# Decay sums read back from device memory instead of picking products, and the state's product in two column tiles

## The reference, cut to what matters

```
dt  = softplus(dt + dt_bias);  dA = dt * (-exp(A_log))        # per token and head, 8 heads
A_cs = cumsum(dA)                                             # over the tokens of a chunk
Lmat = exp(A_cs[l] - A_cs[s]) for l >= s, else 0
Y_diag = sum_s (C_l . B_s) Lmat[l, s] xdt[s]                  # xdt = x * dt
states = sum_s B_s exp(A_cs[-1] - A_cs[s]) xdt[s]
S = S * exp(A_cs[-1]) + states
Y_off  = (C_l . S_before) * exp(A_cs[l])
```

## Time and profile before

| | |
|---|---|
| median of 3 runs | 996.51 us (996.26 to 999.14) |
| profiled execution | 1000.16 us, of which span 998.4 us |
| PE / DVE / ACT / POOL busy | 91% / 79% / 60% / 34% |
| mean granted TensorE clock | 0.97 |

### The profile page before, as it was taken

One profiled execution on the slowest core, in us unless ns is written; L12 is line 12 of the kernel. 1 busy time (PEld: TensorE's weight loads), 2 busy tenths in 40 slices (PEclk: granted clock), 3 DMA queues, 4 the chain that ended last, 5 costly groups with the idle time before them and its releaser, 6 DMA issues.

```text
span 998.4 us, 17980 instructions
## 1 busy us (share of the span) xinstructions
PE 909.1 (91%) x6560; PEld 786.0 (79%) x6560; DVE 789.2 (79%) x2079; ACT 599.2 (60%) x1013; POOL 338.6 (34%) x346
## 2 busy tenths in 40 slices
PE   1556797999999999999999999999999999999987
PEld 0445695888888788888888798878888798888887
DVE  6898777898879988898879988898879888886132
ACT  5955847574737665674737565674838565672222
POOL 2022233334252424334152424234152524234332
PEclk9767799999999999999999999999999999999999
DMA  7300000000001000000001000000000000000000
GB/s 225 124 1 11 1 12 1 12 11 2 11 2 32 1 12 1 11 23 1 12 1 33 1 11 1 11 23 1 12 1 33 2 11 2 5 18 1 1 22 11
DMA packets 14087, 17.70 MB, mean 18 GB/s; under 512 B 1712, under 2 KB 10416, under 8 KB 14000
## 3 DMA queue, kind: packets, MB, share of 16 engines
q1 hardware_dynamic: 13136, 16.53, 5.4%
q10 hardware_dynamic: 864, 0.03, 0.0%
HBM read 12.36 MB, written 4.19 MB: 17 GB/s over the span
## 4 chain that ended last, share of the span: by engine, by line
PE 58%; DVE 22%; ACT 7%; issue 6%; POOL 5%; DMA 1%; SPq 1%; DVEq 0%; POOLq 0%; ACTq 0%
PE fb L1073 23%; PE mb L1073 14%; PE db L1073 11%; DVE xc L882 7%; PE mb L1193 2%; DVE lmat L856 2%; DVE hid L990 2%; DVE lmat L901 2%; POOL yg L557 2%; DMA wd_raw<-in_packed 1%; PE mb L1174 1%; PE mb L1199 1%; PE mb L1184 1%; POOL hl L569 1%; ACT xc L651 1%
## 5 line engine op out<-in xcount | busy, mean ns | idle before, releaser
L569 POOL TENSOR_TENSOR hl<-hid,hl 128x512 fp32r<-128x512 f32 (+1 forms) x144 | 169.5, 1178 | 407.9 <-ACT hl L705 407.7
L1073 PE MATMUL fb<-x1t,wg 128*128 128x512 f32 (+1 forms) x864 | 215.9, 386 | 5.3 <-DVE x1t L984 5.3
L1073 PE MATMUL db<-wd,hl 128*128 128x256 f32 x1536 | 216.6, 289 | 2.2 <-POOL hl L569 2.0
L1073 PEld LDWEIGHTS db<-wd,hl 128*128 128x128 f32 x1536 | 197.4, 189 | 17.8 <-issue 10.1
L1073 PE MATMUL fb<-x1t,wu 128*128 128x512 f32 (+1 forms) x864 | 206.1, 375 | 3.3 <-ACT hid L698 3.3
L1073 PEld LDWEIGHTS fb<-x1t,wu 128*128 128x128 f32 x864 | 153.6, 192 | 36.7 <-ACT hid L698 4.8
L1073 PEld LDWEIGHTS fb<-x1t,wg 128*128 128x128 f32 x864 | 146.3, 193 | 30.9 <-DVE x1t L984 6.7
L990 DVE TENSOR_TENSOR hid<-fb,hid 128x512 f32<-128x512 f32 (+1 forms) x144 | 90.2, 627 | 78.1 <-PE fb L1073 67.6
L705 ACT ACTIVATE hl<-hid 128x512 fp32r<-128x512 f32 (+1 forms) x144 | 83.6, 581 | 106.1 <-DVE hid L990 77.8
L882 DVE SCALAR_TENSOR_TENSOR xc<-raw,cw,xc 128x256 f32<-128x256 f32 x288 | 132.9, 529 | 9.6 <-ACT xc L651 8.3
L698 ACT ACTIVATE hid<-fb 128x512 f32<-128x512 f32 (+1 forms) x144 | 78.1, 548 | 84.8 <-PE fb L1073 81.1
(11 more groups left out here) (150 smaller groups left out, 1360.4 us busy)
## 6 DMA issues: line engine op xcount, KB each, us to landing
xin<-in_u SPq DMA_DIRECT2D x16, 256.0 KB, 2.7
out<-xb SPq DMA_DIRECT2D x16, 256.0 KB, 2.2
wg_raw<-in_packed SPq DMA_DIRECT2D x4, 256.0 KB, 13.2
wg_raw<-in_scales SPq DMA_DIRECT2D x4, 256.0 KB
wu_raw<-in_packed SPq DMA_DIRECT2D x4, 256.0 KB, 13.6
wu_raw<-in_scales SPq DMA_DIRECT2D x4, 256.0 KB
wd_raw<-in_packed SPq DMA_DIRECT2D x4, 256.0 KB, 13.2
wd_raw<-in_scales SPq DMA_DIRECT2D x4, 256.0 KB
```

The source lines that it names most:

```text
L569: pool.tensor_tensor(hl[:, hs, n % 2, 1, :], hid[:, hs, n % 2, :], hl[:, hs, n % 2, 0, :].bitcast(F32), ALU.subtract).then_inc(s["lo"], 1)
L1073: last = pe.matmul(ps, lhs(a, k), rhs(b, k), start=start and n == 0, stop=stop and n == len(todo) - 1, skip_group_check=check)
```

## The change

1. `pick`, `t3`, `seg` and their products go. `da` is now 128 wide with 16 filled columns, `decays` is one copy of the sums from PSUM to `csr` in SBUF, and `ct` is one float32 product of `csr` with 16 columns of the identity, into the same bank as `cs`.
2. SP stores the 16 rows of `csr` (8 KB) in device memory, waits until they have landed, and reads them back twice, 8 rows each (4 KB), each read spread over all 128 partitions straight into `lmat` (512 KB each). It does so for each half in its own queue, between the loads of x and the stores of the result.
3. `sums` waits for both reads and takes the last column from `lmat`, one instruction more. `decay_sums` works in place in `lmat`, so it reads SBUF and not PSUM.
4. `st` is two matmuls of 64 output partitions each.
5. The Mamba table has 42 uses of the three banks in place of 52.

```diff
@@ ORDER["pe"] (FIRST likewise)
-        gu:0< cs:0 gu:1< ct:0 gu:2< dn:0< gu:3< dn:1< seg:0 seg:1 seg:2 dn:2< xtr:0 gu:4< gb:0 yo:0 seg:3 gu:5<
+        gu:0< cs:0 gu:1< ct:0 gu:2< dn:0< gu:3< dn:1< dn:2< xtr:0 gu:4< gb:0 yo:0 gu:5<
...
+            def spread_rows(i, j):
+                if not there("cs", j, i):
+                    return
+                n = halves_before(i, j)
+                sp.wait_ge(s["cs_read"], count("cs_read", i, j))
+                sp.dma_start(rows[n % 2], csr[0:2 * HEADS, :]).then_inc(rows_stored, 16)
+                sp.wait_ge(rows_stored, 16 * n + 16)
+                for c in range(2):
+                    if n == 0:
+                        sp.wait_ge(wi_ready, 2)
+                        sp.wait_ge(wi_z_ready, 1)
+                    else:
+                        sp.wait_ge(s["yd"], count("yd", i, 2 * j + c - 2))
+                    sp.dma_start(lmat[:, c, :, :].rearrange("p h l -> p (h l)"),
+                                 rows[n % 2, HEADS * c:HEADS * c + HEADS, :].rearrange("h l -> (h l)").partition_broadcast(P)
+                                 ).then_inc(rows_spread[c], 16)
...
+            for i in range(NBLK + 1):
+                for j in range(2):
+                    spread_rows(i, j)
+                    next_x(i, j)
+                if i > 0:
+                    store(i - 1, (i - 1) % 2)
...
             def decay_sums(i, par, k):       # ACT; DVE likewise
-                act.wait_ge(s["ct_read"], count("ct_read", i, k // 4))
-                if h0 == 0:
-                    wait_before(act, "yd", i, k // 2 - 2)
-                act.wait_ge(s["seg"], count("seg", i, k))
+                act.wait_ge(s["sums"], count("sums", i, k // 4))
...
-                    last = act.activation(lmat[:, c, h0 + h, :], m_bank["seg", k][:, CH * h:CH * h + CH], ACT.Relu,
+                    last = act.activation(lmat[:, c, h0 + h, :], lmat[:, c, h0 + h, :], ACT.Relu,
...
             def decays(i, par, j):
-                ps = m_bank["cs", j][0:96, 0:CH]
                 dve.wait_ge(s["cs"], count("cs", i, j))
-                link("cs_link", i, 3 * j, dve.tensor_copy(t3[:], ps))
-                dve.tensor_tensor(rest3[0:64, :], ps[0:64, :], t3[0:64, :], ALU.subtract).then_inc(s["cs_read"], 1)
...
+                if halves_before(i, j) > 0:
+                    dve.wait_ge(rows_stored, 16 * halves_before(i, j))
+                dve.tensor_copy(csr[:], m_bank["cs", j][:, 0:CH]).then_inc(s["cs_read"], 1)
             def sums(i, par, j):
...
+                dve.tensor_copy(ct_[:, 0, :], m_bank["cs", j][:, CH:CH + 2 * HEADS]).then_inc(s["ct_read"], 1)
+                for c in range(2):
+                    dve.wait_ge(rows_spread[c], 16 * halves_before(i, j) + 16)
+                dve.tensor_copy(ct_[:, 2, :].rearrange("p (c h) -> p c h", c=2), lmat[:, :, :, CH - 1])
                 dve.wait_ge(s["ct_read"], count("ct_read", i, j))
...
             def ct(i, par, j):
...
+                pe.matmul(m_bank["cs", j][:, CH:CH + 2 * HEADS], csr[:], ident[:, 0:2 * HEADS], start=True,
                           stop=True).then_inc(s["ct"], 1)
...
-                pe.matmul(m_bank["st", q][:], gb[:, 2 + c, :], xdd[:], start=True, stop=True).then_inc(s["st"], 1)
+                for n0 in range(0, NSTATE, HD):
+                    last = pe.matmul(m_bank["st", q][n0:n0 + HD, :], gb[:, 2 + c, n0:n0 + HD], xdd[:], start=True, stop=True)
+                last.then_inc(s["st"], 1)
```

More of the change, by code:

```diff
@@ L181 @@
                 decays=1, ct=1, sums=1, exps=1,
-                seg=4, decay_sums=4, decay_matrix=4, ip=3, taps=3, conv=3, silu=3, z=3, gate=3, gb=1, gb_copy=1,
+                decay_sums=4, decay_matrix=4, ip=3, taps=3, conv=3, silu=3, z=3, gate=3, gb=1, gb_copy=1,
                 decayed_products=2, xtr=2, xdt=2, yo=2, yoff=2, yd=2, st=2, state=2, ydiag=2, square=2, yt=2,
@@ L278, in build @@
         yt = sb("yt", [P, 2, KI, CH], F32R)
-        da = sb("da", [P, 3, 32])
-        t3 = sb("t3", [96, CH], BF16)
-        rest3 = sb("rest3", [96, CH])
+        da = sb("da", [P, CH])
+        csr = sb("csr", [P, CH])
         ct_ = sb("ct_", [P, 3, 2 * HEADS])
@@ L331, in build @@
         out_stored = sem("out_stored")
+        rows_stored = sem("rows_stored")
+        rows_spread = [sem(f"rows_spread{c}") for c in range(2)]
         small_loaded = sem("small_loaded")
@@ L362, in build @@
             var4=1, rstd4=1, d_read=1, outs=2,
[L363 removed]
+            ln1_link=4, dt_link=12, conv_link=30, out_link=24, fin_link=3)
         s = {name: sem("s_" + name) for name in per_block}
@@ L398, in drive, with halves_before @@
             run(LAST[engine], NBLK, 1)
+        rows = nc.dram_tensor("rows", (2, 2 * HEADS, CH), F32, kind="Internal").ap()
+        def halves_before(i, j):
+            return 2 * i + j - 1
         u_v = u.rearrange("b (h c p) d -> (b h) p c d", c=2, p=P)
@@ L460, in load_x, with next_x @@
                 sp.dma_start(xin[:, j, :, :], src).then_inc(x_loaded[j], 16)
[L462 to L467, removed]
+            def next_x(i, j):
+                if there("ln2", 2 * j + 1, i + 1) and (i, j) != (0, 0):
+                    sp.wait_ge(s["attn"], count("attn", i, 2 * j + 1))
+                    load_x(i + 1, j)
+            def spread_rows(i, j):
[14 more added lines that the diff above has]
+                                 ).then_inc(rows_spread[c], 16)
             load_x(0, 1)
-            rows = in_proj.rearrange("(k p) n -> p k n", p=P)
-            sp.dma_start(wi_raw[:, :, DI:], rows[:, :, DI:]).then_inc(wi_loaded[0], 16)
-            sp.dma_start(wi_raw[:, :, 0:DI], rows[:, :, 0:DI]).then_inc(wi_loaded[1], 16)
+            wi_rows = in_proj.rearrange("(k p) n -> p k n", p=P)
+            sp.dma_start(wi_raw[:, :, DI:], wi_rows[:, :, DI:]).then_inc(wi_loaded[0], 16)
+            sp.dma_start(wi_raw[:, :, 0:DI], wi_rows[:, :, 0:DI]).then_inc(wi_loaded[1], 16)
             for q in range(MATS * PIECES):
@@ L515, in consts @@
                 pool.memset(hist[:], 0.0)
-                pool.memset(upto[:], 1.0)
                 pool.memset(da[:], 0.0)
-                link(pool.memset(pick[:], 0.0))
+                link(pool.memset(upto[:], 1.0))
                 pool.affine_select(out=upto[:], in_=upto[:], compare_op=ALU.is_ge, fill=0.0, base=0,
[L521 to L528, removed]
+                                   pattern=[[1, P]], channel_multiplier=-1).then_inc(consts_ready, 1)
             def wi_split(i, par, _):
@@ L1113, in cs @@
                 bank_read(m_uses, ("cs", j), i)
[L1114 to L1115 removed]
+                pe.matmul(ps[:, 0:CH], da[:], upto[:], start=True, stop=True).then_inc(s["cs"], 1)
             def ct(i, par, j):
[L1118 to L1121 removed]
+                pe.wait_ge(s["cs_read"], count("cs_read", i, j))
+                pe.matmul(m_bank["cs", j][:, CH:CH + 2 * HEADS], csr[:], ident[:, 0:2 * HEADS], start=True,
                           stop=True).then_inc(s["ct"], 1)
[L1124 to L1132 removed]
             def z(i, par, q):
```

66 lines of the change are left out of this document (17 added, 49 removed).

## The result

The changed kernel takes 1000.07 us (median of 20 runs, 998.49 to 1002.18). Beside it the kernel before took 996.33 us (20 runs, 994.57 to 1000.89). The ratio is 1.0034, 95% interval 1.0026 to 1.0043: slower by 2.6 to 4.3 us. Its profiled execution took 1001.04 us, with a span of 999.3 at a mean granted clock of 0.967 of full speed.

The account below looks back on a forecast made before the run. PE was taken to bound most of an iteration, DVE one first-half stretch and the second half to `yt:2`. Start +8.1, iterations -3.9, step 8 -1.3, semaphores +0.6 gave +3.5 on 996.5: 1000.0 us, range 988 to 1020.

Parts of the forecast that it names:

- The landing, 7.3 us: Copy to `csr`, store and both reads: the sums lie in `lmat` 7.3 us after `decays` starts; ends 6.4 and 11.4.
- Rival A: Read-back into `lmat`: spread reads slow, 190 GB/s, data 5.5 us not 3.1; +36, about 1036 us; chance 0.14.
- Start +8.1: Start's three halves: rows 3.2 us late each, `sums` 0.2 longer, partly paid back later; 8.1 us, ends 5 and 20.
- First half of an iteration: no stall: DVE's wait for the rows: reads land by 544.4, DVE asks at 544.7 or later; 0.3 to 1.1 us to spare.
- Second half +0.4: Iteration's second half to `yt:2`: +0.5 stall, +0.2 `sums`, +1.1 POOL, -1.0 `decay_sums`, -0.4 waits; PE's relief unused.
- POOL's collision, +1.1: Second half: one `decay_sums`, now reading SBUF, is held about 1.1 us by POOL's `hl`.
- First half -1.3: Iteration's first half: -0.8 `decays`, -1.0 `decay_sums`, +0.2 `sums` make -1.6, counted as -1.3; ends 0 and -2.9.
- The state's tiles +0.25: State's product on PE: tiles run side by side, 0 behind `yd`, +0.25 us at `st:3` for mode changes.
- Rival C: State's product on PE: column tiles do not run side by side, +0.86 x 3 an iteration; 1015 us; chance 0.12.
- Iteration -0.65, tail -1.3, total +3.5: Whole program: six iterations -3.9, step 8's first half -1.3, start +8.1, semaphores +0.6; together +3.5 us.
- PE idle before `yt:2`: Sign of the prediction in an iteration's second half: PE would idle before `yt:2`, waiting for DVE; no size given.
- Rival B: Reads land 0.6 us sooner, POOL's collision falls into a gap, PE's relief counts; -8, about 988.5 us; chance 0.30.

Follow-up runs that it names:

- b_seg_half: The kernel before with two in place of four picking products for each bank from block 2 on; 995.29 us, ratio 0.9973.
- h_again: Repeat of the kernel before's picking products in blocks 0 and 1, the changed kernel's spread from block 2, full-array state's product throughout; 990.14 us, ratio 0.9938.
- a_again: The changed kernel run once more, nothing altered, for a second profile; 1000.15 us, ratio 1.0032.

## Why the prediction was right, and which of its steps were not

The time was predicted at 1000.0 and measured at 1000.07. That the two agree to 0.1 us is luck: the start and the iterations, the two large terms of the sum, were both off, in opposite directions.

- *The landing, 7.3 us from the start of `decays`.* The three waits of the start put L847 6.9, 6.8 and 7.15 us behind it. Right; the store's 1.9 us were too many (SP issues the reads 1.35 us behind the store) and the reads' 5.0 about right: the median is 5.1, of which the first read takes 3.9. The second lands 1.24 us behind it, 512 KB at 420 GB/s. So two reads are 2.5 us of data and 2.6 of fixed part, where I had 3.1 and 1.9. Rival A (190 GB/s) is dead. By the recorded bounds the latest landing adds up to 11.3, not 11.4.
- *Start +8.1.* The three waits are 2.6, 3.6 and 2.5 us, where I had 3.2 each. The start is 8.2 longer by the two profiles. Over seven executions whose first three halves are those of before (196.0 to 201.0, mean 198.5) and four of the changed kind (206.0 to 209.2, mean 207.8) it is 9.3, in parts of 3.1, 3.3 and 2.8 us. Of the 1.1 and 1.0 us that I let later idle time pay back, 0.1 and 0.6 were paid, if each half would have cost my 3.4.
- *First half of an iteration: no stall.* The wait is 0.1 us at most, but 0.7 once; the spare time of 0.3 to 1.1 us is not there. SP's queue shows why:

```profile
541.16 0.90 SPq L510 DMA_DIRECT2D out<-xb  x2
542.11 0.51 SPq L479 DMA_DIRECT2D rows<-csr  x1
544.28 0.83 SPq L487 DMA_DIRECT2D lmat<-rows  x2
```

  The reads are issued 2.7 us behind the start of `decays`, where they are issued 1.7 us behind it in the second half, without stores ahead. I had the store land 2.4 us behind it (539.3 - 536.93). The rows come 8.0 us behind it here and 7.8 in most iterations, and DVE asks after 7.9.
- *Second half: 0.5 us of stall.* 0.1 us, and 0.7 once.
- *Second half +0.4, because `yt:2` waits for DVE and PE's relief is unused.* This step failed. From `decays:1` to the start of `yt:2` are 23.42 us before and 23.00 changed, -0.4 (in the iteration of the two stretches above). The whole stretch comes to -0.2 with the state's tiles and -0.5 with its product in one piece. From the end of L935 at 617.77 and the start of `yt:2` at 617.83 I read that DVE decides. It was only the last step of a chain in which DVE itself followed PE: b_seg_half gains 0.43 us in this stretch from PE alone, all of it before `yt:2`. It is not all PE either: of PE's relief of 0.93 us, 0.53 came out.
- *POOL's collision, +1.1.* It happens, at the place foreseen and at that size. In the second half twelve of `decay_sums` took 3.50 us:

```profile
605.23 3.50 DVE L858 TENSOR_SCALAR lmat<-lmat,ct_ 128x128 f32<-128x128 f32 x12
```

  in the first half 2.43. What it costs is not shown. With it the twelve take as long as before the change (3.53 from first start to last end), and the most that its absence could win there by the waits above is the 0.4 us that PE newly waits for DVE, an estimate. That DVE's time counts from `sums` on, the changed kernel's one late second half shows (from 709.35): rows 0.7 us late, a stretch of 55.2 in place of 54.5, and PE waiting for `gb`:

```profile
PE mb L1094 <- ACT gb L679: 0.6, 1, 0.6
```

  I had also overlooked a second collision: from block 2 on, in every first half but the last, the sixteenth of `decay_sums` takes 1.06 us beside POOL's L567, and in the last first half two of them are held. The page "SBUF — State Buffer" of the Trainium skill, section "Who interferes with whom", describes the mechanism, and the trace agrees (one of the twelve takes 1.34 us, the others 0.28).
- *First half -1.3.* -1.0, and -1.1 without the tiles. L873's counterpart takes 0.37 us (1.19 before) and `decay_sums` 277 ns (343 before) as foreseen; against them stand the 0.8 us of the collision just named.
- *The state's tiles +0.25.* 0.5: the mechanism and `st:3` (0.35) are right, "nothing behind the diagonal" is not, by 0.13 to 0.16. Rival C (+0.86 each) is dead.
- *Iteration -0.65, tail -1.3, total +3.5.* Over two profiles each, an iteration is 1.05 us shorter and the tail 0.9 (1.5 and 0.3). With the start at 9.3 that makes 9.3 - 6.3 - 0.9 = +2.1 us, where the medians say 2.6 to 4.3. The rest may be what the few starts leave uncertain (they spread over 5.0 and 3.2 us); that my 0.6 for semaphores is in it, nothing shows.
- *PE idle before `yt:2`.* 0.2 us, where the kernel before has none: small, but it is a wait for DVE, and part of what PE's relief lost.

So the total came out because errors met: the start cost 1.2 us more than I had, the iterations gave 2.4 more, and the rest is made up of the tail (0.4 less than I had) and of what these few profiles do not resolve.

Rival B had half of the right reason (PE's relief counts in the second half; POOL's collision did not fall into a gap) and the wrong time. It needed the start at +6.5 and the iteration at -2.1; the iteration is -1.0, without the tiles -1.6.

## What to carry to other kernels

A trip through memory of 7 us cost next to nothing in the steady loop here, where as much other work stood between its two ends, and some 3 us each time in the prologue, where it didn't; so use two paths, and give the loop's reader some work of its own before it asks. Before saying which engine decides a stretch, sum its idle time there: PE's 0.46 us of 54.73 said more than which instruction ended last before one matmul. And work added to an engine to see whether it decides must not fall into that engine's idle time. A pair of column tiles alone between full-array matmuls cost 0.35 us here and won nothing, each tile being one long product.

## What the runs showed of the hardware

- Two reads in one queue, each of 4 KB spread over 128 partitions (512 KB written): the first lands 3.9 us after its issue (median), the second 1.24 us later. An 8 KB store is seen by the queue's owner 1.35 us after its issue.
- Two 256 KB stores just ahead in the same queue make that small store land about 0.8 us later.
- The late landings recur at the same halves from run to run (above), so they are not chance. What they share is a packet of a queue whose kind the profile calls `instruction` (16 KB on q8, 8 KB on q14). The nine profiles with the read-back have 135 halves. In 17 the rows come more than 5.6 us after the first read's issue (median of the changed kernel 5.1), and all 17 have such a packet under way in that time. Of the 78 halves without one none takes longer than 5.6. In all ten halves in which a packet of q8 starts within 0.3 us of the first read's issue, SP's second issue takes 0.8 to 1.4 us in place of 0.43. Of h_again, a long and an ordinary pair of issues, and what the window 645.2 to 646 holds beside the long one (packets, MB, share); the window 757.1 to 757.9 of the ordinary one holds no packet:

```profile
645.28 1.70 SPq L510 DMA_DIRECT2D lmat<-rows  x2
```
```profile
757.19 0.81 SPq L510 DMA_DIRECT2D lmat<-rows  x2
```
```profile
q8 instruction: 1, 0.02, 10.2%
```

  A packet is not enough: 40 halves have one and are not late, and a_again had the slow issue with waits of under 0.2 us. No run moved the packets, so that they make the rows late is what the traces suggest, not what they show.
- The start ends anywhere between 196.0 and 201.0 us for one and the same kernel. That is the whole difference between the two profiled executions of the kernel before (1000.16 and 995.33), and why two single profiles (+0.9 us) said less than the medians (+3.7). Whether the loading of the weights makes it, no run tested.
